# Two-layer graph kernel, between the layers: order of the h1 stores, of the grams, of the first query shift and of the tail

## The reference

```
h = relu(layernorm(x));  x1 = x + layer0(h)      # attention over edges, 8 heads, sums by src
h1 = relu(layernorm(x1)); out = x1 + layer1(h1)
layer1(h1):
  xn  = batchnorm(h1)                            # over all nodes
  agg = segment_sum(xn[src], dst) / max(deg, 1)
  conv = relu(agg @ W_conv + b_conv)
  attn = linear attention with 8 heads over the graph's dense part of 256 places, @ Wo
  return batchnorm(conv + attn + h1)
```

## Time and profile before

| what | value |
|---|---|
| runs | 3578.21, 3585.32, 3591.87 us |
| the profiled execution | 3582.55 us, its span 3580.7 us |
| last sum of layer 0 added | about 1906 us |
| first gather of layer 1 | 2081.48 us |
| first counts of the edge loop | 2101.84 us |
| edge loop | 2104 to 3292 us: PE 886.7, DVE 692.6, GpSimd 724.3 us busy |
| GpSimd in the edge loop | 784 gathers of 946 ns, idle 219.6 us for freed places in 79 waits |

### The profile page before, as it was taken

One profiled execution on the slowest core, in us unless ns is written; L12 is line 12 of the kernel. 1 busy time (PEld: TensorE's weight loads), 2 busy tenths in 40 slices (PEclk: granted clock), 3 DMA queues, 4 the chain that ended last, 5 costly groups with the idle time before them and its releaser, 6 DMA issues. The chain is left out here.

```text
span 3580.7 us, 49452 instructions
## 1 busy us (share of the span) xinstructions
PE 2677.7 (75%) x11244; PEld 1676.7 (47%) x11245; DVE 2438.6 (68%) x4268; ACT 993.4 (28%) x3078; POOL 1869.0 (52%) x1889
## 2 busy tenths in 40 slices
PE   6887367777878787777777777767777787778990
PEld 4554255666656566666666642222223333333440
DVE  9999956766767666666668745555555566566667
ACT  6733334444434444444343510000000000000220
POOL 0000255655555555555556456666666666663667
PEclk8988678998988988988888888988888888899995
DMA  5110366666666666666655856665656565654226
GB/s 182 46 40 34 97 179 181 193 183 187 183 192 180 191 185 182 194 180 180 188 170 192 264 171 176 172 175 172 171 170 179 168 178 171 173 169 148 67 65 246
DMA packets 243499, 588.70 MB, mean 164 GB/s; under 512 B 57744, under 2 KB 82832, under 8 KB 243400
## 3 DMA queue, kind: packets, MB, share of 16 engines
q0 software_dynamic: 133120, 443.52, 43.1%
q1 hardware_dynamic: 110280, 144.14, 12.3%
HBM read 533.43 MB, written 54.10 MB: 164 GB/s over the span
## 5 line engine op out<-in xcount | busy, mean ns | idle before, releaser
L503 POOL DMA_INDIRECT big<-feat_table,idx x880 | 838.9, 953 | 1028.5 <-ACT idx L527 409.0
L1129 POOL DMA_INDIRECT big<-h_table,idx x784 | 741.6, 946 | 478.5 <-issue 224.2
L796 PE MATMUL psA<-big,onehot 128*128 128x260 f32 x1760 | 479.0, 420 | 74.0 <-DVE big L678 50.9
L796 PE MATMUL psB<-big,onehot 128*128 128x260 f32 x1760 | 506.7, 438 | 35.5 <-DVE acc L688 31.9
L553 ACT ACTIVATE big<-big,late_weights 128x65 f32<-128x65 f32 x1760 | 434.2, 341 | 0.0
L796 PEld LDWEIGHTS psA<-big,onehot 128*128 128x128 f32 x1760 | 359.3, 211 | 149.7 <-issue 64.1
L796 PEld LDWEIGHTS psB<-big,onehot 128*128 128x128 f32 x1760 | 363.0, 216 | 111.3 <-DVE acc L688 45.6
L1837 PE MATMUL psB<-big,onehot 128*128 x556 | 307.9, 678 | 105.3 <-issue 57.6
L1837 PE MATMUL psA<-big,onehot 128*128 x556 | 300.1, 661 | 102.2 <-issue 53.1
L527 ACT CAST idx<-minorB 128x8 int32 (+1 forms) x101 | 20.3, 203 | 1159.5 <-DMA big<-h_table,idx 1141.4
L1566 DVE TENSOR_TENSOR acc<-acc,psA 128x512 f32 x278 | 190.7, 686 | 142.8 <-issue 68.5
(11 more groups left out here) (436 smaller groups left out, 3804.7 us busy)
## 6 DMA issues: line engine op xcount, KB each, us to landing
nodes_all<-slot_nodes SPq DMA_DIRECT2D x56, 512.0 KB
big<-feat_table,idx POOLq DMA_INDIRECT x880
feat_table<-big SPq DMA_DIRECT2D x49, 264.0 KB, 2.1
x_table<-acc SPq DMA_DIRECT2D x49, 256.0 KB, 3.6
h_table<-big SPq DMA_DIRECT2D x49, 256.0 KB, 3.8
big<-h_table,idx POOLq DMA_INDIRECT x784
big<-h_table SPq DMA_DIRECT2D x49, 256.0 KB, 2.6
big<-x_table SPq DMA_DIRECT2D x49, 256.0 KB, 4.0
```

Of the source, the lines that this page charges most:

```text
L503: g.indirect_dma_start(ring[:, b.k, q * SB + u, :], None, feat_table, bass.IndirectOffsetOnAxis(ap=idx[:, 2 * b.k + q, u:u + 1], axis=0)). ...
L796: ins = pet.matmul(psum[:, 512 * hf:512 * hf + HALF_W], onehot[:, q, u % SB, :], ring[:, b.k, u, HALF_W * hf:HALF_W * (hf + 1)], start=(u ...
L1129: g.indirect_dma_start(big[:, place:place + D], None, h1_table, bass.IndirectOffsetOnAxis(ap=idx[:, r.c % CHUNK_CYCLE, b:b + 1], axis=0)). ...
```

## The change

- `h1_store_slot`: tile u of h1 (from 2 on) is stored behind x1 tile u + 12 in place of u + 16, so 13 in place of 17 stores wait for the last slot.
- ScalarE: h1 tiles 24 to 27 are made before the wait for the last `select` (they stood behind both `exp_q` and `deviations(5)`); tiles 40 and 41 ahead of the heads; then two tiles of h1 with each of the first heads in place of one with each.
- TensorE: the wait for "slots" stands behind grams 24 and 25; in the heads two grams with each of the first four, one with the fifth, in place of one with each from the second and two at the end.
- VectorE: `shift_q(0)` directly behind the tables, ahead of the copies `keep_kv`. In the tail the clearing (line 1542) and the subtractions of "hat" come ahead of the copy of the shift row; the scaling of `Wc_s` comes behind the release of the edge loop.
- TensorE in the tail: "last" ahead of the shift row.

```diff
@@ -418,7 +418,7 @@
 
         def h1_store_slot(t):
 
-            return min(TILES - 1, 16 + t if t >= NT else 8 + t)
+            return min(TILES - 1, 12 + t if t >= NT else 8 + t)
         QUADS = TILES // 4
         assert TILES == 4 * QUADS + 1
         moment_space = alphas[:, :, :].rearrange("p t c -> p (t c)")[:, P:]
@@ -893,7 +893,7 @@
         KV_EARLY = 5
         SDVE = Steps(sem("att_dve"), ["ones", "v0", "v1", "diag", "sel", "ones_mat"] + [f"mk{h}" for h in hs] +
                      ["km", "kmd", "bk", "mq0", "bq0", "mq1", "bq1"] + [f"kf{h}" for h in hs] +
-                     [f"kv{h}" for h in range(KV_EARLY)] + ["qf0"] + [f"kv{h}" for h in range(KV_EARLY, H)] +
+                     ["qf0"] + [f"kv{h}" for h in hs] +
                      [n for h in hs for n in ([f"qf{h + 1}"] if h < H - 1 else []) +
                       ([f"mq{h + 2}", f"bq{h + 2}"] if h < H - 2 else []) + [f"zd{h}", f"zr{h}", f"at{h}"]] + ["hat0", "hat1"])
 
@@ -1244,6 +1244,8 @@
                 h1_tile(20 + a)
                 exp_k(2 * a)
                 exp_k(2 * a + 1)
+            for t in range(24, 28):
+                h1_tile(t)
             PP.wait(act, f"select{SB - 1}")
             for n, ps in enumerate((psD, psE)):
                 ins = s.copy(nodeB[:, :, n * ROWS1 // 2:(n + 1) * ROWS1 // 2].rearrange("p b r -> p r b"),
@@ -1252,7 +1254,7 @@
             exp_q(0)
             exp_q(1)
             deviations(5)
-            for t in range(24, 32):
+            for t in range(28, 32):
                 h1_tile(t)
             for c in range(CHUNK_CYCLE):
                 put_indices(minorB, c, c, idx3)
@@ -1262,13 +1264,15 @@
             for t in range(36, 40):
                 h1_tile(t)
             deviations(7)
+            for t in range(40, 42):
+                h1_tile(t)
             for h in hs:
                 SPE.wait(act, f"qfT{h}")
                 done(s.copy(qfT[:, h % 2, :, :].rearrange("p t n -> p (t n)"), psC[:, h % 2 * 512:h % 2 * 512 + 512]), f"qfT{h}")
                 if h < H - 2:
                     exp_q(h + 2)
-                h1_tile(40 + h)
-            h1_tile(TILES - 1)
+                for t in range(42 + 2 * h, min(44 + 2 * h, TILES)):
+                    h1_tile(t)
             SPE.wait(act, "aT")
             done(s.copy(attnT.rearrange("p k n -> p (k n)"), psA[:, :]), "aT")
             act.wait_ge(bn1_step, VAR_STEP)
@@ -1472,11 +1476,11 @@
             link(v.tensor_scalar(quad_group, own_chunk[64:65, 3:LOTS1:4], float(64 * SB), None, ALU.add))
             link(v.tensor_scalar(quad_group, quad_group, 2, None, ALU.logical_shift_right))
             PD.done(v.tensor_scalar(quads, quad_group, 1.0, None, ALU.add), "chunks")
+            shift_q(0)
             for h in range(KV_EARLY):
                 x1_upto((43, 45, 47, 49, 51)[h])
                 keep_kv(h)
             x1_upto(TILES + 3)
-            shift_q(0)
             for h in range(KV_EARLY, H):
                 keep_kv(h)
             k = [0]
@@ -1533,23 +1537,21 @@
             step(v.tensor_tensor(shift_c, mean_c, scale_c, ALU.mult))
             step(v.tensor_tensor(shift_c, b1c, shift_c, ALU.subtract))
             v.tensor_copy(shift_wide, shift_c.unsqueeze(2).broadcast_to([P, KD, P])).then_inc(bn1_shift, 1)
-            dve.wait_ge(bn1_ps, 1)
-            step(v.tensor_copy(shift_rows, psD))
-            dve.sem_inc(lot1_added, ADD1_CREDIT - 1)
-            for kk in range(KD):
-                step(v.tensor_scalar(Wc_s[:, kk, :], Wc_s[:, kk, :], scale_c[:, kk:kk + 1], None, ALU.mult), False)
             dve.wait_ge(x1_stored[2], 16 * (TILES - CLEARED[2]))
             step(v.memset(acc_flat[:, CLEARED[2] * ACC_W:], 0.0))
             SACT.wait(dve, "wo")
             SPE.wait(dve, "last")
             for t in range(NT):
                 done(v.tensor_tensor(hattn[:, t, :], hattn[:, t, :], psE[:, :], ALU.subtract), f"hat{t}")
+            dve.wait_ge(bn1_ps, 1)
+            step(v.tensor_copy(shift_rows, psD))
             SDVE.wait(dve, f"hat{NT - 1}")
             dve.wait_ge(acc_cleared, 2)
-            dve.sem_inc(lot1_added, 1)
-
+            dve.sem_inc(lot1_added, ADD1_CREDIT)
             PA.wait(dve, "tiles")
             dve.sem_inc(counts_kept, 1)
+            for kk in range(KD):
+                step(v.tensor_scalar(Wc_s[:, kk, :], Wc_s[:, kk, :], scale_c[:, kk:kk + 1], None, ALU.mult), False)
 
             def add_row(r):
                 dve.wait_ge(counted1, r(1, 1))
@@ -1765,10 +1767,11 @@
                 gram(t)
                 if t < 16 + SB:
                     select(t - 16)
-            PA.wait(pe, "slots")
             for h in hs:
                 gram(24 + 2 * h)
                 gram(25 + 2 * h)
+                if h == 0:
+                    PA.wait(pe, "slots")
                 sum_kv(h)
 
             def turn_q(h):
@@ -1798,10 +1801,8 @@
                 done(ins, f"at{h}")
                 if h < H - 1:
                     turn_q(h + 1)
-                if h >= 1:
-                    gram(39 + h)
-            gram(TILES - 2)
-            gram(TILES - 1)
+                for t in range(40 + 2 * h, min(42 + 2 * h, TILES)):
+                    gram(t)
             SDVE.wait(pe, f"at{H - 1}")
             SACT.wait(pe, f"eq{H - 1}")
             for k in range(KD):
@@ -1815,13 +1816,13 @@
                     ins = pet.matmul(psA[:, t * 512:(t + 1) * 512], attnT[:, k, t * P:(t + 1) * P], Wo_s[:, k, :],
                                      start=(k == 0), stop=(k == KD - 1))
             done(ins, "wo")
+            SACT.wait(pe, "wo")
+            done(pet.matmul(psE[:, :], select_last, hattn[:, NT - 1, :], start=True, stop=True), "last")
             pe.wait_ge(bn1_shift, 1)
             pe.wait_ge(Wc_loaded, 16)
             for k in range(KD):
                 ins = pet.matmul(psD, shift_wide[:, k, :], Wc_s[:, k, :], start=(k == 0), stop=(k == KD - 1))
             ins.then_inc(bn1_ps, 1)
-            SACT.wait(pe, "wo")
-            done(pet.matmul(psE[:, :], select_last, hattn[:, NT - 1, :], start=True, stop=True), "last")
 
             def sum_row(r):
                 pe.wait_ge(onehot1_ready, r(1, 1))
```

## The result

The changed kernel takes 3591.86 us (median of 22 runs, 3576.36 to 3599.54), the kernel before beside it 3576.65 us (22 runs). The ratio is **1.0033**, 95% interval 1.0018 to 1.0047: some 12 us slower, where 4.5 us faster was forecast. The steps up to the heads went nearly as worked out; what came behind them did not.

What follows compares the result with a forecast made beforehand. No engine was full in the edge loop, a ring whose start the sums decide; first counts -0.1 (value sums) + 1.4 (heads) - 5.8 (tail) = -4.5 us gave 3580.8 us, ratio 0.9987, range 3568 to 3591.

Steps and rivals of the forecast that it cites:

- First clearing and lock: Value sums: GpSimd's first clearing moves to about 2006.5 and locks VectorE's key shift, making x1 tile 41 10.7 us late.
- Rival 1: Value sums: the first clearing locks nothing, so the end moves by -15.2 us, to 3570 us; chance 0.16.
- The delay is caught up: Value sums: the chain's gains take up the 10.7 us delay, last copy at 2053.0 against 2053.1; -0.1 us.
- Rival 2: Value sums: the stall is not caught up, last copy +5.9 us, counts +5.5, kernel slower at 3591 us; chance 0.22.
- Heads: Attention heads: 4.34 us with two grams, 2.28 without features and gram; the tail starts 1.4 us later.
- First gather 6.2 us earlier.: Start of the edge loop's gathers: -0.1 from the value sums and -6.1 from the earlier last gram.
- Tail from 12.5 to 6.7 us.: From Wo's end to TensorE's first counts: reordering shortens this stretch, a gain of 5.8 us, bounds 1.8 and 5.8.
- The clearing: Tail, VectorE: the 3.96 us clearing fits beside the product with Wo; uncovered it would cost up to 3.96 us.
- Wo is done at 2089.3: Start of the tail: the copy of Wo's result starts at 2089.32, taken as the point the tail is counted from.
- The sums decide: Edge loop start: the end moves by the same amount as the first counts, -4.5 us, if the loop keeps its length.
- the 4.55 us in hand: Edge loop, first full ring: the 25th gather waits 4.55 us for a freed place, so gathers have that much slack.
- Rival 3: Edge loop: it doesn't keep the shift and takes up the gain, leaving 3585 us; chance 0.16.

Runs made afterwards that it cites:

- clear_late: The change, with GpSimd's first clearing held until VectorE's tables are made; 0.9980 of the kernel before, 0.9954 when repeated on a chip without late signals.
- tail_alone: The kernel before with only the tail of the change (last row ahead of the shift row, clearing behind the reciprocals, one release); ratio 1.0003.
- before_here: The kernel before, unedited, run for its trace on a chip without late signals; 3038.65 us.
- after_fourth: The changed kernel, unedited, in the fourth comparison, on a chip with late signals; 1.0008 of the kernel before (3548.42 us).
- after_third: The changed kernel, unedited, in the third comparison, on a chip without late signals; 0.9983 of the kernel before (3040.79 us).
- rest_held_3: The change with the first clearing behind VectorE's tables and 16 of the first 24 gathers behind Wo, on a chip with late signals; 0.9966.
- tail_undone: The change with TensorE's and VectorE's tail of the kernel before; ratio 1.0042 to the kernel before, on a chip with late signals.
- gathers_held: The change with GpSimd's first gather held until TensorE's signal of Wo; ratio 1.0041 to the kernel before, on a chip without late signals.

## Why the prediction was wrong

- **First clearing and lock** (forecast: from 2006.5, a shift of over 10 us, tile 41 10.7 us late). Right: 2001.14 is +95.2, where 2006.5 was +94.5; 11.00 us, 11.0 us late. The working itself had the last tile near 2007, and the clearing started there. Rival 1 fell; clear_late showed its price without the lock: 8 us here, 9 us where no signal is late (0.9983 to 0.9954). The Trainium skill, SBUF — State Buffer, section "Who interferes with whom", agrees with both places: the query shift of 5.18 us before, and now a key shift that started 1.52 us into a clearing and ended 0.29 us behind its end.
- **The delay is caught up** (forecast -0.1). Right: +0.4; pairs and sums run without a gap at a pitch of 2.68 us from 2032.7 on. Rival 2 fell.
- **Heads** (4.34 us, then 2.28; turn 1.3 us later). Right: 4.32, then 2.39 and 2.23; turn 1.9 us later (+169.9 to +168.0).
- **First gather 6.2 us earlier.** Right: 6.0.
- **Tail from 12.5 to 6.7 us.** Right as a tail: 6.7 us in tail_alone. In the change it took 8.6 us (2102.64 to 2111.26): last row and shift row 2.08 and 4.60 in place of 1.02 and 3.60, with a granted clock of 0.50 from 2094 to 2107, behind TensorE's 14.51 us of idle. The clearing was covered.
- **"Wo is done at 2089.3" and the copy follows.** This is the step that failed. The forecast moved the gathers 6 us ahead and left the signals of the turn and of Wo prompt, as in the profile of before, where no gather was out at the turn and 7 at Wo's end. With 16 out Wo's signal came 13.45 us late; the turn's had already cost 2.5 us, and Wo's slower matmuls 1.6. The sum had nothing for any of the three. The warning stood in the view of waits of before: 596 us that end with "remote", 119 of them in two lines of the edge loop, and the forecast read none of it.
- **"The sums decide", so whatever moves the first counts moves the end.** This failed too. tail_alone took 5.5 us off the counts and gained nothing, because the signals behind the counts came late: the first add was 5.6 us later than before and the 25th gather 0.2. The path from the first counts to the first freed place was taken as fixed, and it wasn't. Where no signal is late the 4.55 us in hand don't exist either: in before_here the 25th gather waits for nothing.
- **Rival 3** (the loop doesn't keep the shift) looks like tail_alone, but its reason, a loop that takes up a gain, isn't what the trace shows. **Rival 2** named 3591 us, beside the 3591.86 measured; that is luck, for the stall it rests on was caught up. Late signals were not among the rivals.

On chips without late signals the ratio is 0.9983, beside the 0.9987 that was forecast. That too is luck: the sum's terms don't hold there. Its first counts come 3.0 us earlier, not 4.5, mostly because Wo took 9.47 in place of 7.13 us; the gathers are 8.9 us earlier at the 24th, and a wait for the sums leaves 5.1 us of it at the 25th.

A version that beats both kernels on both kinds of chip came out of it: rest_held, with the first clearing behind the tables and 16 of the first 24 gathers behind Wo, 0.9966 on a chip with late signals and 0.9965 and 0.9967 on those without. clear_late is better still where no signal is late (0.9954) and perhaps less good where they are (0.9980, on another such chip than rest_held, with intervals that overlap).

## What to carry to other kernels

Before a burst of transfers is moved ahead of a short chain of signals, look in the view of waits for idle time that ends with "remote" or with nothing known: here a signal of the chain was late by up to 14.6 us for a head start of 6, and with 8 of the 24 gathers ahead of it Wo's signal stayed prompt. Where a ring has two sides, an earlier start of one counts only if it reaches the first freed place: read the start of the first transfer that needs one (the 25th gather here), and not only the first instruction of the side that was moved. And compare on more than one chip: the same edit was 1.0033 on one and 0.9983 on another.

## What the hardware showed

**Signals of TensorE 3 to 15 us late.** In four of the six comparisons, traces had 552 to 711 us of "remote" waits, and a long burst of gathers ahead of Wo's end went with a late signal of Wo in 7 traces of 7 (2.8 to 14.6 us); with 0 to 8 gathers ahead Wo's signal was prompt in 5 of 5. The number of gathers is no threshold for other signals: the turn's came 2.5 us late with six out (the change), that of the counts 9.1 us late with 12 out (tail_alone) and at once with 17 out (before). Nor does the hold simply last as long as the burst: it ended with the traffic in the change (copy at 2102.64, traffic until 2101.8), but in after_fourth at 2083.34, 3.8 us ahead of the 24th gather's issue at 2087.18. Why some chips do it and the others don't, whether the matmuls themselves or only their signals are late, and whether other engines' signals are held as well, is open. That the late signals are what makes the change lose on such chips rests on three things: without them it gains (0.9983), with gathers held back Wo's copy is prompt again on the same chip, and the version that combines this with the late clearing is 0.9966. That last step alone was never compared with clear_late on one chip with late signals. Why the change cost 12 us in the first result and 1 and 3 us on the other two chips of this kind is open as well.

The Trainium skill, Perfetto Trace Analysis, section "Tensor Engine Instruction (MATMUL, LD_WEIGHTS)", says that the end of a matmul in a profile is estimated from its size, while the semaphore is pushed only once PSUM has acknowledged the last bytes. The traces agree as far as they go: 13.45 us lie between the recorded end of Wo and the copy that waits for its signal. The end of a TensorE row is no proof that anybody has been told.

**The clock.** The mean granted clock is 0.87 on chips with late signals and 0.94 on the others; that the waits are the reason isn't shown. In the change TensorE stood idle for 14.51 us before the last row and ran it at the lower of its two levels (1.2 and 2.4 GHz; granted 0.50 from 2094 to 2107): 2.08 us in place of 1.02. Wo's 16 matmuls took 7.13 us at the full level and 8.71 to 9.47 where the clock was low for a part of them, as in the change, after_third and rest_held_3, but not in tail_undone or gathers_held_3, and on both kinds of chip; after_fourth around its Wo, by windows:

```profile
2058.00:2068.00 10.00, 6.86 (x40) 5.80 (x40) 5.62 (x24) 2.71 (x5) 7.63 (x8) 0.72 0.82 288
2068.00:2078.00 10.00, 9.27 (x16) 3.75 (x16) 6.64 (x8) 1.79 (x3) 7.79 (x8) 0.77 0.72 216
```

The granted clock there is 0.72 and 0.77, between the two levels because it changed within each window. That cost Wo 1.6 us in the change and up to 2.3 us (after_third), which the forecast had not.
